# Twelve unread matmuls on TensorE in each step of the fusing stage of a gated cross-attention block

## The reference

```python
x = x + tanh(g_xattn[0]) * L0_xattn(layernorm(x), ctx, ctx, ...)      # 16 heads
x = x + tanh(g_ffn[0])   * L0_ffn(layernorm(x), ...)                  # 8 routed experts, top 2, and 2 shared
x = x + tanh(g_xattn[1]) * L1_xattn(layernorm(x), ctx)                # this is in the fusing stage
x = x + tanh(g_ffn[1])   * L1_ffn(layernorm(x), ...)                  # quantised, with a convolution
# L1_xattn: one head over the full width of 512
scores = einsum('bsd,bvd->bsv', hidden, ctx)
probs = softmax(scores, axis=-1)
out = einsum('bsv,bvd->bsd', probs, ctx)
```

## Time and profile before

| | |
|---|---|
| median of 3 runs | 1673.55 us |
| profiled execution, its own time | 1673.33 us |
| its span | 1671.7 us |
| PE busy | 1510.4 us, 90% |
| DVE busy | 1053.8 us, 63% |
| ACT busy | 815.9 us, 49% |
| POOL busy | 743.7 us, 44% |
| mean granted TensorE clock | 0.935 of full |

### The profile page before, as it was taken

One profiled execution on the slowest core, in us unless ns is written; L12 is line 12 of the kernel. 1 busy time (PEld: TensorE's weight loads), 2 busy tenths in 40 slices (PEclk: granted clock), 3 DMA queues, 4 the chain that ended last, 5 costly groups with the idle time before them and its releaser, 6 DMA issues. The chain is left out here.

```text
span 1671.7 us, 24835 instructions
## 1 busy us (share of the span) xinstructions
PE 1510.4 (90%) x8764; PEld 1147.7 (69%) x8764; DVE 1053.8 (63%) x1759; ACT 815.9 (49%) x1448; POOL 743.7 (44%) x666
## 2 busy tenths in 40 slices
PE   6589999999978999989999999988888789999997
PEld 5478788788756888867787788765554455555553
DVE  3468878788728564332332333247996899999995
ACT  2145555555522221213343444325777778888883
POOL 0044344435414675243414100255551878888870
PEclk9789999999978999999999999995766889999998
DMA  3157656666326999735535333459772111111112
GB/s 142 46 182 252 210 207 252 228 212 230 127 85 216 355 356 345 247 120 176 179 105 169 119 107 107 138 145 319 235 258 92 38 39 38 64 63 63 52 51 101
DMA packets 131428, 270.31 MB, mean 162 GB/s; under 512 B 16083, under 2 KB 31443, under 8 KB 129288
## 3 DMA queue, kind: packets, MB, share of 16 engines
q1 hardware_dynamic: 100168, 175.47, 31.2%
q0 software_dynamic: 16624, 62.93, 10.7%
q10 hardware_dynamic: 14544, 30.68, 4.9%
HBM read 145.56 MB, written 122.42 MB: 160 GB/s over the span
## 5 line engine op out<-in xcount | busy, mean ns | idle before, releaser
L243 PE MATMUL e_u_ps<-e_xs,w_shared 128*128 128x512 f32 x720 | 169.4, 396 | 6.4 <-DVE e_sg L1262 6.4
L243 PEld LDWEIGHTS e_u_ps<-e_xs,w_shared 128*128 128x128 f32 x720 | 137.6, 192 | 35.4 <-DVE e_sg L1262 6.5
L2357 PE MATMUL f_banks<-b_xdT,w1h 128*128 128x512 f32 x512 | 146.0, 427 | 14.5 <-POOL b_xdT L2107 9.7
L2133 POOL TENSOR_TENSOR b_h<-b_h,b_srow 128x512 f32<-128x512 f32 x112 | 143.3, 1333 | 26.3 <-ACT b_srow L2169 26.3
L1458 PE MATMUL e_u_ps<-e_w,e_xs 128*128 128x512 f32 x528 | 133.0, 401 | 2.0 <-DVE e_xs L1354 1.2
L2357 PEld LDWEIGHTS f_banks<-b_xdT,w1h 128*128 128x128 f32 x512 | 97.1, 196 | 48.2 <-POOL b_xdT L2107 14.1
L2326 PE MATMUL b_o_ps<-w2q,b_h 128*128 128x512 bf16 x448 | 116.9, 384 | 8.7 <-ACT b_h L2163 8.7
L2158 ACT ACTIVATE b_h<-b_h 128x512 f32<-128x512 f32 x128 | 88.2, 690 | 53.4 <-DVE b_h L2248 52.4
L1362 DVE TENSOR_TENSOR e_hT<-e_r_ps,e_hT 128x256 fp32r<-128x256 f32 x69 | 29.3, 424 | 134.5 <-ACT e_hT L1200 134.5
L1458 PEld LDWEIGHTS e_u_ps<-e_w,e_xs 128*128 128x128 f32 x528 | 95.7, 188 | 23.2 <-DVE e_xs L1354 1.6
L2245 DVE SCALAR_TENSOR_TENSOR b_h<-f_banks,cw,b_h 128x511 f32<-128x511 f32 x128 | 95.2, 744 | 22.1 <-ACT b_h L2152 22.1
(11 more groups left out here) (267 smaller groups left out, 3504.5 us busy)
## 6 DMA issues: line engine op xcount, KB each, us to landing
slots_in_scratch<-e_xs SPq DMA_DIRECT2D x22, 1024.0 KB, 8.3
e_xe<-slots_in_scratch SPq DMA_DIRECT2D x69, 256.0 KB, 2.7
experts_out_scratch<-e_ye ACTq DMA_DIRECT2D x69, 256.0 KB, 2.0
yx_a<-in_w POOLq DMA_DIRECT2D x10, 1024.0 KB, 5.9
xin<-in_x SPq DMA_DIRECT2D x16, 512.0 KB, 5.0
xres<-in_x SPq DMA_DIRECT2D x16, 512.0 KB, 5.3
x_scratch<-x SPq DMA_DIRECT2D x32, 256.0 KB, 3.4
xn_scratch<-xn SPq DMA_DIRECT2D x32, 256.0 KB, 2.0
```

The source lines that it names most:

```text
L243: mm = pe.matmul(n.u_ps[:, (2 * q + j) % 4], ws[q // n.KH][:, pa, at:at + P], xs[:, pb, k], start=(k == 0 and (pa, pb) == PASSES[0]), stop ...
L2133: pool.tensor_tensor(ht, ht, srow[:], ALU.mult).then_inc(u_done, 1)
L2357: mm = pe.matmul(f_ps[:, v % RING], n.w1h[:, k, (c - NV) * P:(c - NV + 1) * P], xdT[:, part, k], start=(k == 0 and part == 0), stop=(k == ...
```

## The change

A function `keep_busy(count)` is added to PE's program in `fuse`. It issues `count` matmuls with the 16-bit identity of 128 x 128 as the stationary operand and the same identity, repeated four times by a stride of zero, as the moving one: 512 columns each. They write PSUM bank `t_ps[:, 0]`, which the scores' inputs have been copied out of by then and which the next step's transposes overwrite. Nobody reads what they write, and they wait for and signal nothing. Each full step (0 to 7) calls it with 12, between the small transposes and the wait for `e_done`: 96 matmuls in all. No other instruction is changed or moved.

```diff
--- before.py
+++ after.py
@@ -1892,6 +1892,11 @@
                     mm = pe.matmul(d_ps[:, j % 2, k], low_half[:, par, j, k * P:(k + 1) * P, 0], ident_h[:], start=True, stop=True)
                 mm.then_inc(dT_full, 1)
 
+            def keep_busy(count):
+
+                for _ in range(count):
+                    pe.matmul(t_ps[:, 0], ident_h[:], ident_h[:].unsqueeze(1).to_broadcast([P, KD, P]), start=True, stop=True)
+
             def first_row():
 
                 pe.wait_ge(sc_done, 1)
@@ -1939,6 +1944,7 @@
                 if outs:
                     out_transposes(s - 2, par, 0)
                     out_transposes(s - 2, par, 1)
+                keep_busy(12)
                 pe.wait_ge(e_done, s * TB + TB)
                 for j in range(TB):
                     mm = pe.transpose(p_ps[0:C, j], pr[:, j], ident[:])
```

## The result

The kernel with the twelve matmuls took 1679.72 us (median of 14 runs, 1673.87 to 1685.36), the kernel before 1673.53 us on the same chip (14 runs, 1665.41 to 1678.92). The ratio is 1.0035, 95% interval 1.0018 to 1.0052: slower, by some 6 us. The forecast was 1672.0 us, and its range ended at 1677.5. The profiled execution of the new kernel took 1676.5 us (span 1674.8), so it is one of the shorter ones; the median run took 3 us more than this trace shows.

The account below looks back on a forecast made before the run. DVE, and POOL's gathers in steps that have them, set the length, with PE just in time. 1673.3 + 0.3 - 0.6 - 1.2 = 1671.8 us; the median lies 0.2 higher, so 1672.0 us, range 1667.0 to 1677.5.

Parts of the forecast that it names:

- The price of the twelve: PE time of one step's twelve matmuls: 2.6 us at clock 1.00 or 5.1 us at 0.50.
- their direct effect in the gap: PE's wait before the transposes of the probabilities: the twelve overrun it by 1.0 us at most, nothing in step 5.
- The clock: PE stays at 1.00 for o(0) and o(1), falling before o(3) in most steps: some 10 us of 20, not 7.
- The rival in which it stays at 1.00: Clock carried over the gap holds through the whole step, removing DVE's product waits in steps 3 to 7: 1667.4 us, chance 0.26.
- Step 0: Twelve start at clock 0.50 and it rises within them: +0.3 us, bounds +3.2 and -1.
- Steps 1 and 2: No DVE wait for o(3); POOL and DVE set the length: 0.
- Step 7: No front part, so DVE really waits for products, and o(3) comes earlier: -1.2 us, bounds +1.0 and -3.3.
- Steps 3 to 6: o(0) and o(1) end earlier, o(3) only 0.1 to 0.2 us: -0.6 us for the four, bounds 0 and -2.4.
- Direct cost in steps 1 to 6: nothing: Overrun of 1.0 us behind the twelve goes into 1.5 us of slack before DVE takes o(0): cost nothing.
- a step in the middle changes its length by more than 0.5 us: Sign that the forecast is wrong; steps 1 to 5 were to keep their 20 us.
- no notice: Rival: clock ignores the twelve; step 0 pays 3.2 us, step 7 1.0 us: 1677.7 us, chance 0.09.
- lost rises: Rival: clock's rise before the scores fails in some steps, 3 to 4 us each: 1675.5 or 1679 us, chance 0.15.

Follow-up runs that it names:

- shift4: Changed kernel plus four matmuls of 128 columns ahead of each step's scores: 1668.32 us, 1672.44 for the kernel before (0.9976).
- out_loop: Changed kernel with the twelve only in steps 0, 1, 2 and 7, none in 3 to 6: 1674.72 us (1.0008 to the kernel before).
- unroll12: Changed kernel with PE's loop over steps 3 to 6 written out straight, twelve kept: 1675.24 us (1.0019 to the kernel before).
- light12: Changed kernel with POOL's gathers fetching 64 of 512 elements per row, so another result: 1672.99 us (1.0012 to the kernel before).
- unroll0: Changed kernel with PE's loop written out straight and no filler: 1671.05 us (1.0004 to the kernel before).
- in_loop: Changed kernel with the twelve only in steps 3 to 6, the loop: 1682.67 us (1.0052 to the kernel before).
- direct0: Changed kernel without filler, y's rows loaded as plain blocks from SP instead of POOL's indirect loads: 1669.77 us (0.9987 to the kernel before).
- narrow6: Changed kernel with six matmuls of 128 columns per step instead of twelve of 512: 1673.47 us (1.0001 to the kernel before).
- narrow: Changed kernel with its twelve matmuls of 128 columns instead of 512 in all eight steps: 1679.36 us (1.0031 to the kernel before).
- series 1 and 2: First two groups of follow-up kernels, each on its own chip beside the kernel before, which took 1673.54 and 1671.49 us.
- six: Changed kernel with six matmuls of 512 columns per step instead of twelve: 1669.53 us (0.9983 to the kernel before).
- unroll6: Changed kernel with PE's loop written out straight and six matmuls per step: 1669.24 us (0.9993 to the kernel before).
- fifteen: Changed kernel with fifteen matmuls of 512 columns per step instead of twelve: 1673.48 us (1.0007 to the kernel before).
- direct12: Changed kernel, twelve kept, y's rows loaded as plain blocks from SP instead of POOL's indirect loads: 1668.34 us (0.9979 to the kernel before).
- series 3: Third group of follow-up kernels (no indirect loads, filler ahead of the scores, nine matmuls), on its own chip; kernel before 1671.76 us.
- nine: Changed kernel with nine matmuls of 512 columns per step instead of twelve: 1669.55 us (0.9980 to the kernel before).
- narrow24: Changed kernel with 24 matmuls of 128 columns per step instead of twelve of 512: 1670.20 us (0.9974 to the kernel before).

## Why the prediction was wrong, step by step

**The price of the twelve** was right: 2.6 us forecast, 2.59 us measured in step 3. So was **their direct effect in the gap** of step 3: the transposes of the probabilities start right behind them, at 1194.83. (For step 5 the working had the clock wrong: it said that it is 1.00 at that point in all steps from 1 on, while the earlier trace rows have 0.50 from 1236.0 and the earlier trace rows the transposes at 1236.48, 1.14 us long.)

**The clock** was under-rated. I expected it to hold for o(0) and o(1), some 10 us of 20 at 1.00. It held for 10 to 14 us in the steps with the low stretch between, and through all of step 7. The rival in which it stays at 1.00 did not come true either: of the 6.4 us that it claimed for steps 3 to 7, steps 6 and 7 win 2.6 us. The Trainium skill's page "TensorE: Matmul & The Clock Gate", in the table "Why this matters for your kernels", asks for no long idle gaps between bursts. The gaps filled here were short ones (1.58 us in step 3), and filling them still changed the clock; and the low stretches of shift4, 5.85 of 6.60 us busy and still at 0.50, show once more that the absence of gaps is not all of it. The prediction also read the rise at 1249.7 us as due to the transposes ahead of it. Output products had kept PE busy ahead of those (12.34 of 13.50 us for both together), so the row does not separate the two, and no run here does.

**Step 0**, +0.3 us: wrong in sign, for a reason of timing. The clock rose at 1130.8, ahead of the twelve, so they and all behind them ran at 1.00, and step 0 to 1 is 2.2 us shorter. A rise ahead of the first filler can't be the filler's doing, so this gain is at least in part luck. What the step's working had in mind, a rise within the twelve, stands in the profiles of out_loop (1140.4 us), unroll12 (1138.1), light12 (1137.7) and shift4 (1140.3): 0-1 is there 17.2, 17.8, 17.9 and 17.9 us, 0.3 to 1.0 us shorter than before's, where +0.3 was forecast. With 18 narrow ones the clock stays at 0.50 until 1149.8 us and the interval keeps its 18.2 us.

**Steps 1 and 2**, 0: right, 20.1 and 19.9 us before and after. They are set by DVE and POOL, as said.

**Step 7**, -1.2 us: right in its mechanism, and the size too small, 25.3 to 23.4 us. In the profile DVE waits 1.57 us for the first product and for none of the others, where it waited 1.74, 0.76 and 0.76 us:

```profile
1283.67 0.75 DVE L1875 SCALAR_TENSOR_TENSOR x<-f_banks,rt,f_x 128x512 f32<-128x512 f32 x1 [1.57 <-PE f_banks L1956]
1285.07 0.73 DVE L1875 SCALAR_TENSOR_TENSOR x<-f_banks,rt,f_x 128x512 f32<-128x512 f32 x1
```

The filler is not the only way to that gain: unroll0, without any, has the clock at 1.00 from 1271.7 to 1295.4 us and 22.6 us for 7-ffn. Of the other kernels that have no filler in step 7, in_loop and direct0 keep 25.3 us; so does narrow6 with 0.5 us of it.

**Steps 3 to 6**, -0.6 us with bounds 0 and -2.4, and ahead of it the sentence **"Direct cost in steps 1 to 6: nothing"**: this is what failed. Measured +5.6, +0.8, +2.0 and -0.7 us. The working allowed a delay of 1 us of the copy and found it hidden by 1.5 us of slack behind it. It took for granted that the copy starts when the transposes end, as it did eight times in eight before. It came up to 5.2 us later, and no slack of this kernel covers that. DVE's waits for products, which were to shrink from 8.6 us to 4, grew:

```profile
DVE x L1875 <- PE f_banks L1956: 11.5, 10, 4.8
```

The rule given for being wrong, "a step in the middle changes its length by more than 0.5 us", named the place. None of the rivals was this one. The slower rivals came out right in sign for other reasons: "no notice" falls to the held clock, "lost rises" to the scores, of which none in a later step took near 7 us (3.69 to 4.22 us in steps 1 to 7). 1675.5 to 1679 us was also about the right size, which is no credit to their mechanism.

What causes a late increment is open. Shown, by kernels that have late copies, is that it needs neither the time of the wide filler (narrow, with 0.83 us and idle time behind), nor the loop on PE (unroll12), nor the full bytes of the gathers (light12); and, on one chip, that it came with the twelve in steps 3 to 6 (in_loop) and not without them (out_loop). With six wide ones the profiles of series 1 and 2 have none (six, unroll6). Not shown is what the kernels without late copies suggest: that the number queued does not decide by itself (18, 24 and fifteen lack it), that taking POOL's indirect loads away removes it (direct12), and that four small matmuls ahead of the scores remove it (shift4). All of these ran in the series that had no late copy at all, one profile each. If the chip is not the reason, shift4 still changes two things together, the place of every later instruction in PE's program and the moment at which the step reaches the gap; which of them counts no run here tells. I had expected first a threshold in the number queued, and the last two series speak against that. One more thing is only inferred: that the 3 us by which the median of the changed kernel lies above its profile are late copies too.

The table "Why this matters for your kernels" of the Trainium skill's page "TensorE: Matmul & The Clock Gate" puts the tail of a semaphore increment, for small matmuls packed side by side, at some tens of ns for a single increment. In the trace of before the increment behind the transposes agrees with that size in all eight steps, 0.01 to 0.02 us behind their end; in the changed kernel 5.2 us are measured, and the measurement decides.

## What to carry to other kernels

A filler that nobody reads can be worth its place where the clock falls in a short gap: 1.2 to 2.1 us of it in each step gave 0.2 to 0.4% here, while 0.5 us gave nothing and fifteen wide ones, 3.2 us, gave nothing either. Try several counts and widths and time each: twelve was 0.35% slower than nothing, while nine wide ones and eighteen narrow ones were faster, and so were the same twelve with four more ahead, on another chip. When a kernel behaves oddly, time that same kernel again beside every variant that is meant to cure it, on the same chip; here that control is missing from series 3 on, and so a cure can't be told from a chip that never had the trouble. When a hand-over between engines is on the path, look in the profile for a consumer that waits though its producer has ended ("remote" as the releaser): such a wait isn't in the length of any instruction, and a sum over durations can't find it.

## What the runs showed of the hardware that I had not expected

- The increment behind PE's last transpose of a group can arrive 2.4 to 6.0 us behind the transpose's modelled end, eight times in five profiled executions, always in a step in which POOL issues indirect loads; five of the eight ended within 0.1 us of the end of POOL's root behind the last load.
- Four of these eight had no recorded instruction fetch within 10 us.
- 18 matmuls of 128 columns, 1.17 us of work in a step, were worth at least as much as six wide ones in 1.46 us (0.9964 and 0.9983, in different series), though six of 128 columns were worth nothing.
- Five profiles of kernels with twelve in the gap and the indirect loads have late copies, yet in different steps (3 and 5 twice, 3 and 4, 5 alone twice), and shift4, with twelve in the gap too, has none; so one profile is not enough to find them or to rule them out.
- PE's clock rose in step 0 before any filler had run in three profiles (changed kernel at 1130.8 us, nine, narrow24), and it stayed at 1.00 through step 7 in one kernel without filler (unroll0): a clock gain seen in one profile is not yet the change's.
